# A group's ten transposes in one run over three PSUM banks, and products on two banks

## The chip, the core and the metric

The kernel runs on one core of one Trainium2 chip. The time is that of the device for one execution of the whole program, in microseconds. Engines are named as the profile names them: PE is TensorE, PEld its weight loads, DVE VectorE, ACT ScalarE, POOL GpSimd and SP SyncE.

## What is computed

A recommendation model scores 2048 samples. Each has 50 items of history; their 128-wide rows are gathered from a table, scored against the sample's target by a small network, weighted by a softmax and summed. Five features and their ten pairwise products make a row of 15 × 128 = 1920 numbers, which goes through two cross layers (1920 × 1920) and three dense layers. Cut to what matters:

```python
x = jnp.concatenate([t, seq_emb, t - seq_emb, t * seq_emb], axis=-1)
scores = (jax.nn.relu(x @ aw1 + ab1) @ aw2 + ab2)[..., 0]
weights = jax.nn.softmax(jnp.where(mask, -1e9, scores), axis=1)
hist_feat = jnp.einsum('bs,bsd->bd', weights, seq_emb)
...
for i in range(2):
    xc = dnn_in * (xc @ cross_K[i] + cross_bias[i]) + xc
h = gelu(ln(xc @ w1 + b1)); h = gelu(ln(h @ w2 + b2)); out = sigmoid(h @ w3 + b3)
```

## The kernel before

The batch is cut into 16 tiles of 128 samples, and these into four chunks of four tiles. An opening prepares the rows of chunk 0 and ends at about 324 us. From then on chunk c is multiplied while the histories of chunk c+1 are worked on; chunk 3 has no history beside it.

**Products.** A chunk has 30 steps (two layers of 15 output blocks; `step`, L698) and then a stage for w1. A step makes one block of 128 outputs for 512 samples, in one PSUM bank of 512 columns: `products` (L560) is called three times in a step, for five of the 15 input blocks each, here called the step's first, second and third block of products. Each input block takes three matmuls (L575 to L577), since weights and inputs are split in a high and a low part. Step n writes bank n % 3 of `xps`; DVE reads it in the next step (`x_scale`, L1237), and `x_end` gives the bank back by the semaphore `bank_free`. The fourth bank (`FCB`, semaphore `bank4_free`) serves the small products and the dense layers. In the w1 stage the four tiles each have one of these four banks.

**A group of history.** A tile's 50 items are five groups of ten. In a step that has a group (`p.grp`; 20 of the 30 steps of chunks 0, 1 and 2, in sets of five with a step between the sets), PE transposes the ten gathered blocks `e`: five behind the first block of products and five behind the second (`transposes`, L487, with u = 0 and 1). Both fives go to the same place, `tps` in `aps`, which is guarded by the semaphore `tp_free`: the second five wait until ACT has copied the first to `eT` (`copy_eT`, L780). DVE multiplies the ten copies by the target (`times_target`, L1099) into `teT`; in the next step `hidden` (L509) multiplies both behind the first block of products, and `score` (L524) comes at the step's end. One step later ACT weighs the ten blocks (`weigh`, L810) and DVE sums them (`history`, L1144). The gathers themselves are issued by POOL (L440), a group at a time, when `history` has freed the place.

**Order on ACT.** It is written out in `step` (L954): weight split for the first block (`unit`, which calls `w_hi`, L855), the softmax's exponentials and ten `weigh`, `x_hi` of the previous step (L880, which waits for DVE's `x_end`), the first copy, `unit` for the second block, in some steps a gelu of the dense layers, the second copy, and `unit` for the third. A `w_hi` works three blocks of products ahead. DVE makes the low part of the same weights (`w_lo`, L1212).

**Dense layers.** In steps 2 to 10 of chunks 1, 2 and 3 the dense layers of the chunk before run in between: `fc_turn1` (L643) behind a first block of products, waiting for the norms of DVE (L1278, semaphore `h1n_ready`) and for `FCB`; its gelu on ACT (L894); `fc_w2` (L651) behind the third block, waiting for that gelu; `fc_bias2` on DVE (L1287), which gives `FCB` back.

Of the kernel before, what the change touches and what calls it, by code (L numbers as in the profile page):

```python
# [12 lines left out]
P = 128  # L13
EMB = 128
# [30 lines left out]
SBUFS = 3  # L45
BANKS = 3
EPS = 1e-5
# [94 lines left out]
def build(nc, idx_d, table_d, cate_d, embT_d, rows_d, cols_d, mmw_d, aw1_d, bil_d, kx_d, w1_d, w2_d, out_d, ntiles):  # L142
    assert sum(TILES) == ntiles
    with ExitStack() as ctx:
# [3 lines left out]
        def ps(name, shape):  # L148
            return ctx.enter_context(nc.psum_tensor(name, shape, F32))
# [8 lines left out]

        xps = ps("xps", [P, BANKS + 1, 512])
        FCB = BANKS  # L160
        mps = xps[:, FCB, :]
        aps = ps("aps", [P, 2 * 512])
        tps = aps[:, 0:SUB * P]
        gps = aps[:, SUB * P:(SUB + 1) * P]
        hps = ps("hps", [P, 2 * 512])
        hsum = hps[:, 0:SUB * P]
        hscore = hps[:, SUB * P:SUB * P + GRP]

        spare = xps[:, 0:2, :].rearrange("p k n -> p (k n)")
        tps2 = spare[:, 0:SUB * P]  # L170
        gps2 = spare[:, SUB * P:(SUB + 1) * P]
        hscore2 = xps[:, 2, 0:GRP]

# [197 lines left out]
        lo_final = X1l[:].rearrange("p t f b -> p (t f b)")  # L371

        def raw_slot(w):
            return w % WRING
# [102 lines left out]
        def _(pe):  # L477
# [8 lines left out]

            def transposes(t, g, u):  # L487
                if u == 0:
                    pe.wait_ge(*landed(t, g))
                pe.wait_ge(tp_free, 1).then_inc(tp_free, -1)  # L490
                for s in range(groups(t)[g][1]):
                    last = nc.tensor.transpose(tps[:, s * P:(s + 1) * P], e_sub(t, g, u, s), ident[:])  # L492
                last.then_inc(tp_ready, 1)
# [113 lines left out]
            def w1_products(c):  # L607
                T = TILES[c]
                assert T > 1
                tiles = [b for b in (0, 1, 3, 2) if b < T]  # L610

                whole = FEATS - FINAL if c == CHUNKS - 1 else FEATS
                for k, b in [(k, b) for k in range(whole) for b in tiles]:
                    if b == 0:
# [12 lines left out]
                    m2 = mm(out, xl, Wh[:, s, 0:H1], start=False, stop=(k == FEATS - 1))  # L627
                    if b == 0:
# [3 lines left out]
                    if b == 1:  # L632
                        m0.then_inc(w_free, 1)
                    if k == FEATS - 1 and b == 0:
# [4 lines left out]
                for b in range(T, BANKS):  # L639
                    pe.wait_ge(bank_free, 1).then_inc(bank_free, -1)  # L640

# [37 lines left out]
            def opening_step(p):  # L679
# [18 lines left out]
            def step(p):  # L698
# [8 lines left out]
                if p.grp:  # L707
                    transposes(*p.grp, 0)
# [50 lines left out]
        def _(act):  # L759
# [19 lines left out]

            def copy_eT(u, n=SUB):  # L780
                act.wait_ge(tp_ready, 1).then_inc(tp_ready, -1)
                act.wait_ge(eT_free, 1).then_inc(eT_free, -1)  # L782
                done(af(eT[:, u, 0:n * P], tps[:, 0:n * P], ACT.Copy))  # L783
                act.sem_inc(tp_free, 1)
                act.sem_inc(eT_ready, 1)
# [147 lines left out]
            def opening_step(p):  # L933
# [6 lines left out]
                if p.grp:  # L940
                    n = groups(p.grp[0])[p.grp[1]][1]
                    copy_eT(0, n)
# [11 lines left out]
            def step(p):  # L954
# [18 lines left out]
                if p.grp:  # L973
                    copy_eT(0)
                if p.gate is not None:
# [71 lines left out]
        def _(dve):  # L1047
# [5 lines left out]
            def images():  # L1053
                dve.wait_ge(img_mm, 1).then_inc(img_mm, -1)
                psum = xps[:].rearrange("p k n -> p (k n)").rearrange("p (t n) -> p t n", n=EMB)

# [180 lines left out]
            def x_scale(c, layer, n):  # L1237
                dve.wait_ge(sum_done, 1).then_inc(sum_done, -1)
                dve.wait_ge(mm_done, 1).then_inc(mm_done, -1)
                v.scalar_tensor_tensor(out=fresh(c, layer, n), in0=by_tile(xps[:, n % BANKS, :], c), scalar=col("cb", layer * FEATS + n),  # L1240
                                       in1=fresh(c, layer, n), op0=ALU.add, op1=ALU.mult).then_inc(scaled, 1)
# [62 lines left out]
            def h1_bias(b):  # L1304
                done(v.tensor_tensor(h1[:, b, :], xps[:, b, :], row("b1"), ALU.add))
                dve.sem_inc(bank_free if b < BANKS else bank4_free, 1)

            def h1_rest(c):
                dve.wait_ge(mm_done, 1).then_inc(mm_done, -1)
                for b in range(1, TILES[c]):  # L1310
                    h1_bias(b)
                if TILES[c] < BANKS:
                    dve.sem_inc(bank_free, BANKS - TILES[c])

# [86 lines left out]
            def w1_stage(c):  # L1401
                for k in range(FEATS):
# [4 lines left out]
                    if k == FEATS - 1 and c + 1 < CHUNKS:  # L1407
                        dve.wait_ge(mm_done, 1).then_inc(mm_done, -1)
                        h1_bias(0)
                    unit(c, BLOCKS + k)  # L1410
# [78 lines left out]
            norm2(T - 1)  # L1489
            if T < BANKS:  # L1490
                dve.sem_inc(bank_free, BANKS - T)
            fc_probs(c)
# [50 lines left out]
```

## Time and profile before

| | us |
|---|---|
| median of 3 runs | 2115.8 |
| lowest, highest | 2112.77, 2117.34 |
| the profiled execution | 2113.03 |
| its span | 2111.2 |
| PE busy | 1928.6 (91%) |
| DVE busy | 1337.5 (63%) |
| ACT busy | 914.2 (43%) |
| POOL busy | 894.6 (42%) |

The span runs from the first to the last instruction; 1.8 us of the execution lie around it. A timeline row gives start, duration, engine, line, operation, tiles, sizes, the number of merged instructions, and in brackets the idle time of the engine before it and what ended that; a name with a q (PEq, DVEq) is the engine's own queue, standing at a semaphore. A matmul's shown duration (0.39 us for 512 columns) is longer than the distance to the next one, as matmuls overlap; distances between starts tell what PE can do.

### The profile page before, as it was taken

To read this page: it belongs to the slowest core of one execution; us is meant where nothing else is said; L and a number is where in the kernel's file an instruction comes from. 1 tells how busy PE (TensorE), PEld (TensorE's weight loads), DVE (VectorE), ACT (ScalarE), POOL (GpSimd) and SP (SyncE) were. 2 spreads that over 40 slices of the span, in tenths; PEclk is the share of its full clock that TensorE was granted. 3 is DMA by queue.
4 is the path that set the end of the run, shared out by engine and by line. 5 is a ranking of instruction groups with operands and counts; after the bars stand their busy time and mean duration, and the time that the engine had idled before them with its cause. 6 is when DMAs were issued, how large, how long until landed. Compare 5 with 4: busy or idle time off the path is not lost. (4 is left out here: it accounts for less than half of the span.)

```text
span 2111.2 us, 32903 instructions
## 1 busy us (share of the span) xinstructions
PE 1928.6 (91%) x9608; PEld 1513.0 (72%) x9608; DVE 1337.5 (63%) x2248; ACT 914.2 (43%) x1987; POOL 894.6 (42%) x854
## 2 busy tenths in 40 slices
PE   1666558999999999999999999999999999999997
PEld 1444336777777887777777886777777888888886
DVE  4555564767777755667777755667777654445553
ACT  1433343454544335654444235654445233322234
POOL 7777776556556511555556501555560000000000
PEclk6766669999999999999999999999999999999998
DMA  5112113334434452334434452334332353333320
GB/s 165 50 48 53 50 50 102 104 100 132 117 110 120 144 192 69 99 90 124 125 105 125 142 184 69 99 94 127 118 109 92 111 175 126 89 99 96 98 68 1
DMA packets 99679, 220.31 MB, mean 104 GB/s; under 512 B 21792, under 2 KB 27184, under 8 KB 99376
## 3 DMA queue, kind: packets, MB, share of 16 engines
q1 hardware_dynamic: 63072, 136.90, 21.3%
q0 software_dynamic: 27136, 55.63, 10.5%
q10 hardware_dynamic: 9296, 25.70, 3.3%
q8 instruction: 80, 1.31, 0.3%
q14 instruction: 95, 0.78, 0.1%
HBM read 205.29 MB, written 12.85 MB: 103 GB/s over the span
## 5 line engine op out<-in xcount | busy, mean ns | idle before, releaser
L440 POOL DMA_INDIRECT e<-in_item_table,idx_all x800 | 843.7, 1055 | 650.9 <-issue 302.1
L1212 DVE TENSOR_TENSOR Wl<-raw,Wh 128x640 fp32r<-128x640 f32 (+1 forms) x411 | 331.9, 807 | 267.0 <-DVEq L1211 265.8
L855 ACT ACTIVATE Wh<-raw 128x640 fp32r<-128x640 f32 (+1 forms) x411 | 296.0, 724 | 470.6 <-ACTq L854 467.6
L575 PE MATMUL xps<-X0h,Wh 128*128 128x512 f32 x900 | 364.1, 404 | 1.4 <-PEq L573 1.4
L575 PE MATMUL xps<-X1h,Wh 128*128 128x512 f32 x900 | 359.4, 399 | 0.0
L577 PE MATMUL xps<-X0h,Wl 128*128 128x512 f32 x900 | 351.6, 391 | 0.0
L576 PE MATMUL xps<-X0l,Wh 128*128 128x512 f32 x900 | 351.2, 390 | 0.0
L577 PE MATMUL xps<-X1h,Wl 128*128 128x512 f32 x900 | 351.0, 390 | 0.0
L576 PE MATMUL xps<-X1l,Wh 128*128 128x512 f32 x900 | 350.7, 390 | 0.0
L814 ACT ACTIVATE e<-e,pw 128x128 f32<-128x128 f32 x800 | 242.9, 388 | 15.5 <-ACTq L139 15.5
L577 PEld LDWEIGHTS xps<-X0h,Wl 128*128 128x128 f32 x900 | 169.1, 188 | 37.0
L577 PEld LDWEIGHTS xps<-X1h,Wl 128*128 128x128 f32 x900 | 168.9, 188 | 36.4
L575 PEld LDWEIGHTS xps<-X0h,Wh 128*128 128x128 f32 x900 | 169.5, 188 | 35.4 <-issue 3.5
L575 PEld LDWEIGHTS xps<-X1h,Wh 128*128 128x128 f32 x900 | 169.2, 188 | 33.6 <-issue 1.0
L576 PEld LDWEIGHTS xps<-X1l,Wh 128*128 128x128 f32 x900 | 169.4, 188 | 32.2
L576 PEld LDWEIGHTS xps<-X0l,Wh 128*128 128x128 f32 x900 | 169.7, 189 | 31.1
L1151 DVE TENSOR_REDUCE hist<-e 128x128 f32<-128x1280 f32 (+1 forms) x65 | 155.9, 2399 | 49.5 <-DVEq L1149 49.5
L783 ACT ACTIVATE eT<-aps 128x640 f32<-128x640 f32 x141 | 98.1, 696 | 165.2 <-ACTq L782 164.6
L1103 DVE TENSOR_TENSOR teT<-eT,tT 128x1280 f32<-128x1280 f32 x79 | 117.7, 1490 | 65.2 <-DVEq L1101 65.1
L517 PE MATMUL hps<-eT,A 128*64 128x512 f32 (+2 forms) x640 | 135.9, 505 | 20.0 <-PEq L511 19.9
L492 PE MATMUL aps<-ident,e 128*128 128x128 f32 x700 | 109.3, 289 | 40.4 <-issue 30.4
L521 PE MATMUL hps<-teT,A 128*64 128x512 f32 (+2 forms) x640 | 133.2, 496 | 0.0
(159 smaller groups left out, 2196.7 us busy)
## 6 DMA issues: line engine op xcount, KB each, us to landing
raw<-in_cross_K SPq DMA_DIRECT2D x360, 320.0 KB
raw<-in_w SPq DMA_DIRECT2D x51, 256.0 KB
e<-in_item_table,idx_all POOLq DMA_INDIRECT x800, 2.5
dnn_scratch<-dn ACTq DMA_DIRECT2D x12, 960.0 KB
x1f<-dnn_scratch ACTq DMA_DIRECT2D x3, 2048.0 KB, 9.6
x1f<-dnn_scratch ACTq DMA_DIRECT2D x3, 1792.0 KB, 15.2
e<-in_w SPq DMA_DIRECT2D x9, 256.0 KB, 4.6
dn<-in_embT SPq DMA_DIRECT2D x1, 1024.0 KB, 5.3
```

The lines of the kernel that those rows point to most:

```text
L440: nc.gpsimd.indirect_dma_start(out=dst, out_offset=None, in_=table, in_offset=bass.IndirectOffsetOnAxis(ap=idx_all[:, t, s:s + 1], axis=0) ...
L492: last = nc.tensor.transpose(tps[:, s * P:(s + 1) * P], e_sub(t, g, u, s), ident[:])
L517: last = mm(hsum[u * HID:(u + 1) * HID, a:b], A12[:], eT[:, u, a:b], start=True, stop=False)
L521: last = mm(hsum[u * HID:(u + 1) * HID, a:b], A3[:], teT[:, u, a:b], start=False, stop=True)
L575: m0 = mm(out, wh, Xh[:, 0:T, k, :], start=(k == 0), stop=False)
L576: m1 = mm(out, wh, Xl[:, 0:T, k, :], start=False, stop=False)
L577: m2 = mm(out, wl, Xh[:, 0:T, k, :], start=False, stop=(k == FEATS - 1))
L814: last = af(x, x, ACT.Copy, scale=pw[:, g % 2, s:s + 1])
L855: af(Wh[:, split_slot(w), 0:n], raw[:, rs, 0:n], ACT.Copy).then_inc(hi_done, 1)
L1103: v.tensor_tensor(teT[:].rearrange("p u (s b) -> p (u s) b", b=P), eT[:].rearrange("p u (s b) -> p (u s) b", b=P), tT[:, par:par + 1, :].t ...
L1151: done(v.tensor_reduce(hist[:] if g else acc[:, par, :], x, AX.X, ALU.add))
L1212: v.tensor_tensor(Wl[:, rs, 0:n], raw[:, rs, 0:n], Wh[:, slot, 0:n].bitcast(F32), ALU.subtract).then_inc(lo_done, 1)
```

## The change

The PSUM is one tensor of eight banks. Products alternate between banks 0 and 1; bank 2 is `FCB`; banks 3, 4 and 5 are a place for ten transposes (1280 columns, two and a half banks); 6 and 7 are as before. In a step with a group all ten transposes stand behind the first block of products (`transposes10`), and one ACT instruction of 128×1280 copies them (`copy_eT10`), where the first copy was. Behind the second block none is left. In the w1 stage tile 3 uses bank 3, guarded by `tp_free`, and the tiles are taken in the order 0, 2, 3, 1, so that the bank last used by a step comes last. The opening keeps its form with five and five (`transposes`, `transposes2`), and only its banks have other numbers. The core of the diff:

```diff
-BANKS = 3
+BANKS = 2
+FCB = 2
+TURN = 3
+W1_ORDER = (0, 2, 3, 1)
...
+        turns = flat[:, TURN * 512:(TURN + 3) * 512]
+        tps10 = turns[:, 0:GRP * P]
...
+            def transposes10(t, g):
+                pe.wait_ge(*landed(t, g))
+                pe.wait_ge(tp_free, 1).then_inc(tp_free, -1)
+                for i in range(GRP):
+                    last = nc.tensor.transpose(tps10[:, i * P:(i + 1) * P], e_sub(t, g, i // SUB, i % SUB), ident[:])
+                last.then_inc(tp_ready, 1)
...
-                out = by_tile(xps[:, n % BANKS, :], c)
+                out = by_tile(xps[:, (layer * FEATS + n) % BANKS, :], c)
...
-                tiles = [b for b in (0, 1, 3, 2) if b < T]
+                tiles = w1_order(c)
...
+                    elif k == 0 and b == FCB:
+                        pe.wait_ge(bank4_free, 1).then_inc(bank4_free, -1)
                     elif k == 0:
-                        pe.wait_ge(bank4_free, 1).then_inc(bank4_free, -1)
+                        pe.wait_ge(tp_free, 1).then_inc(tp_free, -1)
...
                 if p.grp:
-                    transposes(*p.grp, 0)
+                    transposes10(*p.grp)
 
                 products(p.chunk, p.layer, p.n, 1)
-                if p.grp:
-                    transposes(*p.grp, 1)
-                elif p.swing is not None:
+                if p.swing is not None:
                     head_turn()
...
+            def copy_eT10():
+                act.wait_ge(tp_ready, 1).then_inc(tp_ready, -1)
+                act.wait_ge(eT_free, 2).then_inc(eT_free, -2)
+                done(af(eT[:].rearrange("p u n -> p (u n)"), tps10, ACT.Copy))
+                act.sem_inc(tp_free, 1)
+                act.sem_inc(eT_ready, 2)
...
                 if p.grp:
-                    copy_eT(0)
+                    copy_eT10()
                 if p.gate is not None:
                     tail_gate()
                 unit(c, 3 * k + 1)
                 if T and 2 <= k < T + 2:
                     fc_gelu1(k - 2)
 
-                if p.grp:
-                    copy_eT(1)
-                elif p.swing is not None:
+                if p.swing is not None:
                     copy_tT(p.swing)
...
             def h1_rest(c):
                 dve.wait_ge(mm_done, 1).then_inc(mm_done, -1)
-                for b in range(1, TILES[c]):
+                for b in w1_order(c)[1:]:
                     h1_bias(b)
```

On PE, in step 9 of chunk 1, from the end of the first block of products to the dense layers' last product (`fc_w3`, on `dn,cols`); L517 and L521 are `hidden`, L492 the transposes. Before:

```order
L521 MATMUL hps<-teT,A 64x128 x2
L492 MATMUL aps<-ident,e 128x128 x5
L575 MATMUL xps<-X0h,Wh 128x512
...
L577 MATMUL xps<-X0h,Wl 128x512
L492 MATMUL aps<-ident,e 128x128 x5
L675 MATMUL xps<-dn,cols 4x128 x8
L575 MATMUL xps<-X0h,Wh 128x512
```

And after:

```order
L532 MATMUL psum<-teT,A 64x128 x2
L503 MATMUL psum<-ident,e 128x128 x10
L586 MATMUL psum<-X0h,Wh 128x512
...
L588 MATMUL psum<-X0h,Wl 128x512
L685 MATMUL psum<-dn,cols 4x128 x8
L586 MATMUL psum<-X0h,Wh 128x512
```

The five transposes that stood behind the second block now stand with the first five, one block of products earlier, and what follows the second block no longer has transposes ahead of it.

On ACT, in step 2 of chunk 1, from `x_hi` (on `X1h`) over the copies (to `eT`), the weight split (to `Wh`) and the gelu (to `dn`) to the third block's split. Before:

```order
L880 ACTIVATE X1h<-x1f 128x4x128
L783 ACTIVATE eT<-aps 128x640
L855 ACTIVATE Wh<-raw 128x640
L894 ACT_TABLE_LOAD
L894 ACTIVATE dn<-xps,cols 128x128 x4
L783 ACTIVATE eT<-aps 128x640
L855 ACTIVATE Wh<-raw 128x640 x2
```

And after:

```order
L895 ACTIVATE X1h<-x1f 128x4x128
L791 ACTIVATE eT<-psum 128x1280
L870 ACTIVATE Wh<-raw 128x640
L909 ACT_TABLE_LOAD
L909 ACTIVATE dn<-psum,cols 128x128 x4
L870 ACTIVATE Wh<-raw 128x640 x2
```

The second copy is gone from behind the gelu, and the first is twice as wide and stands ahead of the weight split and the gelu.

## Rows read from the trace of the kernel before

**Rows 1.** The page: its head, and PE's busy time.

```profile
span 2111.2 us, 32903 instructions
PE 1928.6 (91%) x9608; PEld 1513.0 (72%) x9608; DVE 1337.5 (63%) x2248; ACT 914.2 (43%) x1987; POOL 894.6 (42%) x854
```

**Rows 2.** Waits of PE, 340 to 2085: total us, times, longest.

```profile
PE aps L492 <- PEq L490: 9.9, 9, 1.8
PE xps L648 <- PEq L646: 6.5, 2, 3.5
```

**Rows 3.** Timeline of PE, transposes behind a second block, without a wait.

```profile
811.64 0.39 PE L577 MATMUL xps<-X0h,Wl 128*128 128x512 f32 x1
811.88 0.71 PE L492 MATMUL aps<-ident,e 128*128 128x128 f32 x5
812.34 0.48 PE L575 MATMUL xps<-X0h,Wh 128*128 128x512 f32 x1
812.66 0.39 PE L576 MATMUL xps<-X0l,Wh 128*128 128x512 f32 x1
```

**Rows 4.** Timeline of PE, step 9 of chunk 1, the second five transposes.

```profile
928.66 0.39 PE L577 MATMUL xps<-X0h,Wl 128*128 128x512 f32 x1
930.52 0.74 PE L492 MATMUL aps<-ident,e 128*128 128x128 f32 x5 [1.47 <-PEq L490]
```

**Rows 5.** Timeline of ACT in the same step.

```profile
929.06 0.61 ACT L880 ACTIVATE X1h<-x1f 128x512 fp32r<-128x512 f32 x1
929.58 0.68 ACT L783 ACTIVATE eT<-aps 128x640 f32<-128x640 f32 x1
```

**Rows 6.** Lines by form, ACT, whole span: copies of five transposes, of one.

```profile
L783 ACT ACTIVATE eT<-aps 128x640 f32<-128x640 f32 x139 | 97.2, 699 | 161.8 <-ACTq L782 161.3
L798 ACT ACTIVATE tT<-aps 128x128 f32<-128x128 f32 x13 | 3.6, 278 | 35.2 <-ACTq L797 35.2
```

**Rows 7.** Timeline of ACT and PE, step 3 of chunk 1: gelu, copy, split, `fc_w2`.

```profile
829.27 1.51 ACT L894 ACTIVATE dn<-xps,cols 128x128 f32<-128x128 f32 x4
831.20 0.71 ACT L783 ACTIVATE eT<-aps 128x640 f32<-128x640 f32 x1 [0.42 <-ACTq L782]
832.32 0.74 ACT L855 ACTIVATE Wh<-raw 128x640 fp32r<-128x640 f32 x1 [0.41 <-ACTq L854]
833.14 1.89 PE L656 MATMUL xps<-w,dn 128*128 128x256 f32 x8
```

**Rows 8.** Timeline of DVE and PE from that step to the next `fc_turn1`.

```profile
832.23 1.49 DVE L1103 TENSOR_TENSOR teT<-eT,tT 128x1280 f32<-128x1280 f32 x1 [1.49 <-DVEq L1101]
833.64 0.82 DVE L1212 TENSOR_TENSOR Wl<-raw,Wh 128x640 fp32r<-128x640 f32 x1
842.61 0.63 PE L648 MATMUL xps<-ident,dn 128*128 128x128 f32 x4 [3.04 <-PEq L646]
```

**Rows 9.** Timeline of PE and DVE, steps 1 and 2 of chunk 2.

```profile
1271.15 0.52 PE L492 MATMUL aps<-ident,e 128*128 128x128 f32 x3 [1.37 <-PEq L490]
1276.43 1.92 DVE L1278 TENSOR_SCALAR dn<-dn,fmv,frstd 128x512 f32<-128x512 f32 x4 [0.15 <-DVEq L139]
1278.55 0.60 PE L648 MATMUL xps<-ident,dn 128*128 128x128 f32 x4
```

**Rows 10.** Timeline of PE, last group of chunk 0: waits for its gathers.

```profile
661.77 0.74 PE L492 MATMUL aps<-ident,e 128*128 128x128 f32 x5 [0.55 <-issue]
```

**Rows 11.** Timeline of DVE and PE: a bank's read, and the step after.

```profile
700.31 0.75 DVE L1240 SCALAR_TENSOR_TENSOR x0f<-xps,cols,x0f 128x512 f32<-128x512 f32 x1
705.16 0.39 PE L575 MATMUL xps<-X1h,Wh 128*128 128x512 f32 x1
```

**Rows 12.** Busy time by stretch: PE, PEld, DVE, ACT, POOL, PEclk, DMA share, GB/s.

```profile
822.27:825.65 3.38, 3.38 (x26) 1.90 (x26) 0.29 (x1) 3.38 (x11) 0.00 (x0) 1.00 0.00 0
842.61:847.62 5.01, 5.01 (x25) 2.65 (x26) 0.54 (x1) 3.55 (x11) 2.66 (x3) 0.66 0.20 52
941.72:945.49 3.77, 3.77 (x31) 2.46 (x30) 1.51 (x4) 3.55 (x11) 2.10 (x3) 1.00 0.07 19
```

More of the change, by code:

```diff
@@ L156, in build @@
         img_d = nc.dram_tensor("img_scratch", (ntiles, P, EMB), F32, kind="Internal").ap()
-        xps = ps("xps", [P, BANKS + 1, 512])
-        FCB = BANKS
+        flat = ps("psum", [P, 8 * 512])
+        xps = flat[:, 0:4 * 512].rearrange("p (k n) -> p k n", n=512)
         mps = xps[:, FCB, :]
[L162 to L165, printed above, removed]
+        turns = flat[:, TURN * 512:(TURN + 3) * 512]
+        tps10 = turns[:, 0:GRP * P]
+        tps = turns[:, 0:SUB * P]
+        gps = turns[:, SUB * P:(SUB + 1) * P]
+        hscore2 = turns[:, 2 * 512:2 * 512 + GRP]
+        hps = flat[:, 6 * 512:8 * 512]
         hsum = hps[:, 0:SUB * P]
         hscore = hps[:, SUB * P:SUB * P + GRP]
-        spare = xps[:, 0:2, :].rearrange("p k n -> p (k n)")
+        spare = flat[:, 0:2 * 512]
         tps2 = spare[:, 0:SUB * P]
         gps2 = spare[:, SUB * P:(SUB + 1) * P]
-        hscore2 = xps[:, 2, 0:GRP]
         x_at = -(-nc.sbuf_base // 32) * 32
@@ L371, in build, with w1_order @@
         lo_final = X1l[:].rearrange("p t f b -> p (t f b)")
+        def w1_order(c):
+            return [b for b in W1_ORDER if b < TILES[c]]
         def raw_slot(w):
@@ L484, in images, with transposes @@
                 last.then_inc(img_mm, 1)
-            def transposes(t, g, u):
-                if u == 0:
-                    pe.wait_ge(*landed(t, g))
+            def transposes(t, g):
+                pe.wait_ge(*landed(t, g))
                 pe.wait_ge(tp_free, 1).then_inc(tp_free, -1)
                 for s in range(groups(t)[g][1]):
-                    last = nc.tensor.transpose(tps[:, s * P:(s + 1) * P], e_sub(t, g, u, s), ident[:])
+                    last = nc.tensor.transpose(tps[:, s * P:(s + 1) * P], e_sub(t, g, 0, s), ident[:])
+                last.then_inc(tp_ready, 1)
+            def transposes10(t, g):
+                pe.wait_ge(*landed(t, g))
+                pe.wait_ge(tp_free, 1).then_inc(tp_free, -1)
+                for i in range(GRP):
+                    last = nc.tensor.transpose(tps10[:, i * P:(i + 1) * P], e_sub(t, g, i // SUB, i % SUB), ident[:])
                 last.then_inc(tp_ready, 1)
@@ L609, in w1_products @@
                 assert T > 1
-                tiles = [b for b in (0, 1, 3, 2) if b < T]
+                tiles = w1_order(c)
                 whole = FEATS - FINAL if c == CHUNKS - 1 else FEATS
                 for k, b in [(k, b) for k in range(whole) for b in tiles]:
-                    if b == 0:
+                    if b == tiles[0]:
                         pe.wait_ge(w_ready, 1).then_inc(w_ready, -1)
@@ L627, in w1_products @@
                     m2 = mm(out, xl, Wh[:, s, 0:H1], start=False, stop=(k == FEATS - 1))
-                    if b == 0:
+                    if b == tiles[0]:
                         m0.then_inc(split_free, 1)
@@ L631, in w1_products @@
                             m1.then_inc(x0_free, 1)
-                    if b == 1:
+                    if b == tiles[1]:
                         m0.then_inc(w_free, 1)
-                    if k == FEATS - 1 and b == 0:
+                    if k == FEATS - 1 and b == tiles[0]:
                         m2.then_inc(mm_done, 1)
@@ L637, in w1_products @@
                     m2.then_inc(mm_done, 1)
-                for b in range(T, BANKS):
-                    pe.wait_ge(bank_free, 1).then_inc(bank_free, -1)
             def fc_turn1(j, bank=FCB):
@@ L690, in opening_step @@
                 if p.grp:
-                    transposes(*p.grp, 0)
+                    transposes(*p.grp)
                     transposes2(*p.grp, p.swing is not None)
@@ L707, in step @@
                 if p.grp:
-                    transposes(*p.grp, 0)
+                    transposes10(*p.grp)
                 products(p.chunk, p.layer, p.n, 1)
-                if p.grp:
-                    transposes(*p.grp, 1)
-                elif p.swing is not None:
+                if p.swing is not None:
                     head_turn()
@@ L777, in head_fetch, with copy_eT @@
                 act.dma_start(S[:, b, 3, :], img_d[t]).then_inc(img_landed[b], DMA)
-            def copy_eT(u, n=SUB):
+            def copy_eT10():
[4 more added lines that the diff above has]
+                act.sem_inc(eT_ready, 2)
+            def copy_eT(n):
                 act.wait_ge(tp_ready, 1).then_inc(tp_ready, -1)
                 act.wait_ge(eT_free, 1).then_inc(eT_free, -1)
-                done(af(eT[:, u, 0:n * P], tps[:, 0:n * P], ACT.Copy))
+                done(af(eT[:, 0, 0:n * P], tps[:, 0:n * P], ACT.Copy))
                 act.sem_inc(tp_free, 1)
@@ L941, in opening_step @@
                     n = groups(p.grp[0])[p.grp[1]][1]
-                    copy_eT(0, n)
+                    copy_eT(n)
                     copy_eT2(p.swing, n)
@@ L1054, in images @@
                 dve.wait_ge(img_mm, 1).then_inc(img_mm, -1)
-                psum = xps[:].rearrange("p k n -> p (k n)").rearrange("p (t n) -> p t n", n=EMB)
+                psum = flat[:, 0:ntiles * EMB].rearrange("p (t n) -> p t n", n=EMB)
                 def wide(q):
@@ L1239, in x_scale @@
                 dve.wait_ge(mm_done, 1).then_inc(mm_done, -1)
-                v.scalar_tensor_tensor(out=fresh(c, layer, n), in0=by_tile(xps[:, n % BANKS, :], c), scalar=col("cb", layer * FEATS + n),
+                v.scalar_tensor_tensor(out=fresh(c, layer, n), in0=by_tile(xps[:, (layer * FEATS + n) % BANKS, :], c), scalar=col("cb", layer * FEATS + n),
                                        in1=fresh(c, layer, n), op0=ALU.add, op1=ALU.mult).then_inc(scaled, 1)
@@ L1305, in h1_bias @@
                 done(v.tensor_tensor(h1[:, b, :], xps[:, b, :], row("b1"), ALU.add))
-                dve.sem_inc(bank_free if b < BANKS else bank4_free, 1)
+                dve.sem_inc(bank_free if b < BANKS else bank4_free if b == FCB else tp_free, 1)
             def h1_rest(c):
                 dve.wait_ge(mm_done, 1).then_inc(mm_done, -1)
-                for b in range(1, TILES[c]):
+                for b in w1_order(c)[1:]:
                     h1_bias(b)
-                if TILES[c] < BANKS:
-                    dve.sem_inc(bank_free, BANKS - TILES[c])
             def opening_step(p):
@@ L1408, in w1_stage @@
                         dve.wait_ge(mm_done, 1).then_inc(mm_done, -1)
-                        h1_bias(0)
+                        h1_bias(w1_order(c)[0])
                     unit(c, BLOCKS + k)
@@ L1489, in _ @@
             norm2(T - 1)
-            if T < BANKS:
-                dve.sem_inc(bank_free, BANKS - T)
             fc_probs(c)
```

## The prediction

> **What bounds the kernel now.** I read the page first: PE is busy for 1928.6 of 2111.2 us [rows 1]. What is missing lies mostly in the opening before 324 us, which the change leaves as it is. From 340 us to 2085 us PE hardly stands: the view of waits has nine waits at the transposes, 9.9 us together and at most 1.8, two at `fc_turn1`, 6.5 us, and one for gathers [rows 2, 10]. So only two kinds of things can shorten the run: instructions that leave PE's stream, or those waits. The nine waits are what this change meets. The timeline shows one of them [rows 4, 5]: in step 9 of chunk 1 ACT comes to its first copy only at 929.58, behind ten `weigh` and `x_hi`, and PE, which has been through its second block of products at 928.66, stands until 930.52, because the second five transposes go to the place that this copy empties. PE is not waiting for data that it needs, but for its own output place.
>
> **Part 1, PE's own work.** Sixty groups lose a second run of five transposes and get five more in the first. What an extra run costs is read where none waits [rows 3]: from the last product at 811.64 to the first of the next block 0.70 us, and 0.32 to the one after it, against 0.23 and 0.23 between products (811.64 to 811.88 is about that distance): 1.02 - 0.46 = 0.56 us for the run. What a transpose costs inside a run is the difference between five [rows 3] and four (the run of L648) [rows 9]: 0.71 - 0.60 = 0.11 us, so five more cost 0.55. Saved per group: 0.01 to 0.02 us, about 1 us over 60 groups. A switch from products to transposes and back is nearly free here; this part of the change gives next to nothing. Bounds: 0 (a run is worth its transposes) to 60 x 0.09 = 5 us (if the longer distance at re-entry, 0.32 against 0.23, goes whole). I take 1.0. In chunk 0 even that is lost: its last group waits for its gathers [rows 10], which POOL issues one behind the other, so PE meets the same landing later or earlier. That leaves 0.7.
>
> **Part 2, the nine waits.** They go, as no transposes stand behind a second block any more, and the ten in the first run need a place whose copy was made a step earlier. The idle column understates one of them: 928.66 to 930.52 is 1.86 us where 0.24 is usual [rows 3, 4], so 1.62 us are lost where the row says 1.47; 0.15 more for each. One of the nine, 0.3 us, lies in chunk 0 ahead of the wait for gathers and is worth nothing by the argument above. Eight are left: 9.6 + 8 x 0.15 = 10.8 us. Small ones that the view leaves out may add 0.3: 11.1 us.
>
> **What is late next?** ACT is as late as before and only nobody stands for it there. I followed what stands behind it. The ten transposes end 0.55 us later than five did. The copy of 1280 columns: the line through 128 columns, 278 ns, and 640, 699 ns [rows 6] gives 699 + 640 x 0.82 = 1.23 us, at most twice 0.70 = 1.40 and at least, if the second half came at no cost, 0.70; I take 1.23, since the slope is of the same operation. So in a step with a gelu (8 of these steps have a group) the gelu ends 0.55 + 1.23 - 0.71 = 1.07 us later, at 831.85 instead of 829.27 + 1.51 = 830.78, and PE wants it at 833.14 for `fc_w2` [rows 7]. The margin is 2.4 us before and 1.3 us after: nothing to pay, and if the copy took 1.40, 1.1 us would be left. Were the cover gone, each 0.1 us over it would cost 8 x 0.1 us. The split `w_hi` behind the first copy comes 0.5 to 1.1 us later, and works three blocks of products ahead, over 10 us.
>
> In step 1 of chunks 1 and 2 one wait does come. There DVE's norms feed `fc_turn1` of step 2. Its first norm ends at 1276.43 + 1.92/4 = 1276.91 [rows 9]; behind the later split DVE is late by 1.23 - 0.68 = 0.55, so 1277.46. PE would stand there at 1278.55, less the 1.5 us that it no longer loses at 1271.15 [rows 9], so at 1277.05: 0.4 us of new wait, and by the same rows of chunk 1 some 0.2. I take 0.6 us back.
>
> **Part 3, DVE and the bank of the dense layers.** DVE stands 1.49 us in this step before `times_target` for the second copy [rows 8]. This goes, since both halves now come with the first. The split behind it is then the next to be late: ACT reaches it without the second copy at 831.85 + 0.41 = 832.26 instead of 832.32, ready at 833.0, where DVE took it at 833.64 [rows 7, 8]. So DVE's row of work from there on, up to `fc_bias2`, comes 0.6 us earlier, and `fc_turn1` of step 4, which stands 3.04 us for the bank that this releases [rows 8], stands less by as much. Two such waits, 3.0 and 3.5 us [rows 2]: I take 2 x 0.5 = 1.0 us; bounds 0 and 2 x 1.5.
>
> **Part 4, two banks instead of three.** A step now needs the bank that DVE reads in the step just before. The tightest place I found has the read end at 701.06 and the next step start at 705.16 [rows 11]: 4.1 us of slack. Price nothing; below nothing it can't go, since a third bank releases no one here. The w1 order and the wait on `tp_free` there meet banks idle for several us: nothing. The gathers of chunks 1 and 2 land well ahead; only the group of [rows 10] waits.
>
> **Sum**, against the profiled execution: 2113.0 - 0.7 - 11.1 + 0.6 - 1.0 = 2100.8 us. That execution lies 2.8 us under the median of the three runs, 2115.8, and near the lowest; a median of the changed kernel should then lie between 2100.8 and 2103.6. **I say 2102.**
>
> **The skill against the trace.** Windows that hold nothing but small work between products show how the clock takes it: 3.77 us from `hidden` over the bilinear products to the transposes at a granted clock of 1.00, the 2.4 GHz level [rows 12]. The Trainium skill, TensorE: Matmul & The Clock Gate, Part 4 on the PE-mode transpose, says that transposes don't count as activity of the engine in the way that other matmuls do; by it a longer run of transposes speaks against this change, and the second rival would be the likely case. The trace so far doesn't bear that out.
>
> **Rivals.** *First, the waits come back (0.14).* PE is up to 1.8 us earlier and stands for the same late ACT or DVE a little further on, at `hidden`, `score` or `fc_w2`. For it: ACT is as busy as ever and its first copy starts later. Against it: the margin of 1.3 us [rows 7], and that each of these places lies a whole block of products further on. If all of part 2 came back: 2113 - 1 = 2112; if half, 2107. *Second, slower (0.05): the clock falls behind the longer run.* The same instructions, from `fc_turn1` to the next product, took 3.38 us at clock 1.00 and 5.01 us at 0.66, after the wait of 3.04 us [rows 8, 12]: 1.63 us a fall. The longest stretch of small work grows from 3.77 to 4.3 us, the usual one by the same 0.55. It decides from 12.1/1.63 = 8 falls on, where the gain is eaten, and from 10 the kernel is slower by over 0.2%; at all 60 groups it would be 2101 + 98 = 2199. Against it: 3.77 us did no harm. *Third, more than I say (0.09):* that one fall in the middle vanishes with the shorter wait ahead of it (1.6 us) and the two waits at `fc_turn1` go whole (5.5 us more): 2094. *The change doing nothing on PE* is the first rival with parts 1 and 3 at 0, 2113.
>
> **Chances.** My forecast 0.72, the rivals 0.14, 0.05 and 0.09. The range from 2095 to 2111 takes in the bounds of the copy, of part 1 and of part 3, a first rival by half, and the spread of the runs; it leaves out full return, the clock case and the far end of the third. A measurement can tell about 0.2%, 4.2 us, from no change, so faster means under 2111.6: 0.84; same 0.11; slower 0.05.
>
> **What would show it.** In the profile after: no wait of PE at the ten transposes but the one for gathers near 661 us; ten transposes 1.25 us long between `hidden` and the second block; one copy of 1280 columns at 1.2 to 1.3 us, 60 times; DVE's wait ahead of `times_target` shorter by more than half; the waits at `fc_turn1` near 2.5 and 3.0 us, and two small new ones, 0.2 to 0.4 us, at `fc_turn1` in step 2; the clock at 1.00 from 330 us to the end but for that one fall. The forecast is wrong if the copy takes over 2 us, if PE stands at `fc_w2`, or if windows over the new runs show a clock under 1.

## Result and the profile after

| | us |
|---|---|
| the kernel before, median of 5 runs | 2116.82 (2112.77 to 2118.65) |
| the changed kernel, median of 5 runs | 2102.35 (2101.58 to 2107.81) |
| ratio, with its 95% interval | 0.9934 (0.9922 to 0.9945) |
| the profiled execution of the changed kernel | 2104.58, span 2102.6 |

Five later runs of the changed kernel, beside their own runs of the kernel before, gave 0.9949 (0.9937 to 0.9962), median 2107.89. Single runs of one kernel on one chip differ by 3 to 11 us (`bias_again` below, 2100.29 to 2111.11), so differences of 1 or 2 us are read below from profiles, not from medians.

The page and the waits of PE from 340 to 2085 us, the answer to [rows 1, 2]:

```profile
span 2102.6 us, 32483 instructions
...
PE psum L658 <- PEq L656: 6.9, 4, 3.0
PE psum L658 <- PEq L654: 2.6, 1, 2.6
PE psum L503 <- issue: 0.6, 1, 0.6
```

The nine waits at transposes are gone. Only the wait for gathers is left at the ten (L503, as in [rows 10]), and `fc_turn1` (L658) now waits four times instead of twice in the steps. The row of 2.6 us belongs to the program's last stage, at 2084 us, where the kernel before has a wait of its own (2.92 us at 2092.8) that lay just outside the stretch.

One run of ten transposes with nothing else in it, and the copies, the answer to [rows 3, 6]:

```profile
792.33 0.39 PE L588 MATMUL psum<-X0h,Wl 128*128 128x512 f32 x1
792.56 1.25 PE L503 MATMUL psum<-ident,e 128*128 128x128 f32 x10
793.57 0.48 PE L586 MATMUL psum<-X0h,Wh 128*128 128x512 f32 x1
793.89 0.39 PE L587 MATMUL psum<-X0l,Wh 128*128 128x512 f32 x1
...
L791 ACT ACTIVATE eT<-psum 128x1280 f32<-128x1280 f32 x60 | 73.9, 1232 | 24.7 <-ACTq L790 24.6
```

From 792.33 to 793.57 are 1.24 us and to the next 0.32, less two product distances of 0.23: 1.10 us for ten, where five took 0.56. Two fives are 1.12. The wide copy takes 1232 ns.

Step 3 of chunk 1, the answer to [rows 7, 8], ACT, DVE and PE:

```profile
829.77 1.51 ACT L909 ACTIVATE dn<-psum,cols 128x128 f32<-128x128 f32 x4
831.70 0.74 ACT L870 ACTIVATE Wh<-raw 128x640 fp32r<-128x640 f32 x1 [0.42 <-ACTq L869]
832.54 1.89 PE L666 MATMUL psum<-w,dn 128*128 128x256 f32 x8
832.58 0.82 DVE L1225 TENSOR_TENSOR Wl<-raw,Wh 128x640 fp32r<-128x640 f32 x1 [1.00 <-DVEq L1224]
841.76 0.92 PE L658 MATMUL psum<-ident,dn 128*128 128x128 f32 x4 [2.80 <-PEq L656]
```

The gelu ends at 831.28, 1.26 us ahead of `fc_w2`. DVE stands 1.00 us ahead of the low part for the third block, now for ACT's split.

Where the time went is told by the two middle chunks, each stretch from a chunk's first product to the next chunk's; columns as in [rows 12]. Before:

```profile
778.25:1251.44 473.19, 465.46 (x2396) 365.98 (x2394) 328.46 (x545) 230.01 (x496) 225.51 (x212) 1.00 0.40 118
1251.44:1723.78 472.34, 463.73 (x2396) 365.25 (x2394) 326.48 (x538) 230.24 (x496) 165.25 (x156) 1.00 0.37 111
```

After:

```profile
778.37:1246.22 467.85, 464.58 (x2395) 366.52 (x2394) 328.66 (x545) 225.64 (x476) 227.85 (x212) 1.00 0.40 120
1246.22:1715.40 469.18, 465.47 (x2395) 367.59 (x2394) 326.52 (x538) 226.33 (x476) 167.33 (x156) 0.99 0.37 111
```

Chunk 1 is 5.3 us shorter and chunk 2 only 3.2. Behind the difference is TensorE's granted clock, which goes from its upper level (2.4 GHz, shown as 1.00) to its lower one (1.2 GHz) for some microseconds, here called a fall. Windows over the small work from `fc_turn1` in step 4 on, chunk 1 and chunk 2 of the changed kernel:

```profile
841.76:847.50 5.74, 5.74 (x31) 3.10 (x32) 0.95 (x2) 3.55 (x11) 3.61 (x4) 0.70 0.21 57
1310.20:1317.30 7.10, 7.10 (x31) 3.98 (x32) 1.13 (x3) 3.55 (x11) 2.66 (x3) 0.56 0.13 37
```

After the waits of 2.80 and 3.00 us PE worked at a granted clock of 0.70 and 0.56, between its two levels on the mean of the stretch. Without a fall this work takes 3.38 [rows 12] + 0.55 = 3.93 us to the next product; it took 5.56 and 6.88 in the two chunks. So the falls cost 1.6 and 3.0 us. Before, chunk 1 had one of 1.6 us and chunk 2 none, though its wait there was the longest, 3.50 us (granted clock 1.00 from 1312 to 1325 us). In `two_banks` below, with these same two waits, the clock fell behind both (granted clock 0.50 from 843.75 to 849.5 us and from 1318.73 to 1324, the small work behind the waits). So the 3.0 us that were given back in chunk 2 are a matter of the execution and not of the change.

### The profile page after: what moved, and what is told of

The parts are those of the page before. It is cut to its first block and busy times, and to the rows that moved or that the text cites. A ratio compares the mean times of both kernels' runs of the same rounds, so it can differ in the third digit from the quotient of the medians.

```text
span 2102.6 us, 32483 instructions
## 1 busy us (share of the span) xinstructions
PE 1933.7 (92%) x9608; PEld 1519.9 (72%) x9608; DVE 1336.6 (64%) x2248; ACT 903.2 (43%) x1927; POOL 894.0 (43%) x854
## 5 line engine op out<-in xcount | busy, mean ns | idle before, releaser
L586 PE MATMUL psum<-X0h,Wh 128*128 128x512 f32 x900 | 361.4, 402 | 1.2 <-PEq L584 1.2
L586 PE MATMUL psum<-X1h,Wh 128*128 128x512 f32 x900 | 357.1, 397 | 0.0
L587 PE MATMUL psum<-X0l,Wh 128*128 128x512 f32 x900 | 351.4, 390 | 0.0
L588 PE MATMUL psum<-X0h,Wl 128*128 128x512 f32 x900 | 351.1, 390 | 0.0
L587 PE MATMUL psum<-X1l,Wh 128*128 128x512 f32 x900 | 350.9, 390 | 0.0
L588 PE MATMUL psum<-X1h,Wl 128*128 128x512 f32 x900 | 350.4, 389 | 0.0
L586 PEld LDWEIGHTS psum<-X0h,Wh 128*128 128x128 f32 x900 | 169.4, 188 | 36.5 <-issue 3.3
L588 PEld LDWEIGHTS psum<-X0h,Wl 128*128 128x128 f32 x900 | 169.1, 188 | 36.8
L587 PEld LDWEIGHTS psum<-X1l,Wh 128*128 128x128 f32 x900 | 169.2, 188 | 32.9
L587 PEld LDWEIGHTS psum<-X0l,Wh 128*128 128x128 f32 x900 | 169.6, 188 | 32.0
L528 PE MATMUL psum<-eT,A 128*64 128x512 f32 (+2 forms) x640 | 139.1, 516 | 18.9 <-PEq L522 18.5
L1116 DVE TENSOR_TENSOR teT<-eT,tT 128x1280 f32<-128x1280 f32 x79 | 117.4, 1487 | 41.2 <-DVEq L1114 41.2
```

The costliest lines, as they stand in the source:

```text
L528: last = mm(hsum[u * HID:(u + 1) * HID, a:b], A12[:], eT[:, u, a:b], start=True, stop=False)
L586: m0 = mm(out, wh, Xh[:, 0:T, k, :], start=(k == 0), stop=False)
L587: m1 = mm(out, wh, Xl[:, 0:T, k, :], start=False, stop=False)
L588: m2 = mm(out, wl, Xh[:, 0:T, k, :], start=False, stop=(k == FEATS - 1))
L1116: v.tensor_tensor(teT[:].rearrange("p u (s b) -> p (u s) b", b=P), eT[:].rearrange("p u (s b) -> p (u s) b", b=P), tT[:, par:par + 1, :].t ...
```

## The experiments

Each kernel is the changed one with the edit shown, unless its name says otherwise. Medians of different chips differ, so the ratio to the kernel before on the same chip is what counts.

### Only the banks: `two_banks`

The five and five transposes into one place, with their two copies, are put back; the two product banks and the w1 order stay.

```diff
-                    transposes10(*p.grp)
+                    transposes(*p.grp, 0)
...
                 products(p.chunk, p.layer, p.n, 1)
-                if p.swing is not None:
+                if p.grp:
+                    transposes(*p.grp, 1)
+                elif p.swing is not None:
...
```

> The changed kernel with one part undone: the ten transposes are again five behind the first and five behind the second block of products, into one place, with two copies of 640 columns; products stay on two banks, with the new order in the w1 stage. My theory (the gain is the eight waits of PE for that place): the nine waits are back, 9.5 to 10 us in the view of waits, and the time is that of the kernel before, 2115 to 2118 us, ratio 0.999 to 1.001. Rival (two banks themselves give or cost time): a ratio away from 1, below 0.998 if the banks carry the gain, above 1.002 if PE now stands at bank_free.

Measured: 2115.96 us, ratio 0.9997 (0.9988 to 1.0006), as expected. PE's waits from 340 to 2085 us:

```profile
PE psum L497 <- PEq L495: 9.8, 9, 1.8
PE psum L659 <- PEq L657: 6.6, 2, 3.5
PE psum L497 <- issue: 0.6, 1, 0.6
```

These are rows 2 and 10 of the kernel before again, in number and size. No wait at `bank_free` is among them. Two banks and the new order cost nothing and give nothing that 0.1% would show.

### The wait away, nothing merged: `own_banks`

Four transposes behind the first block in bank 3, six behind the second in banks 4 and 5, with semaphores and a copy of their own. (Two places of five would share bank 4 between a write of PE and a read of ACT with nothing to order them, so four and six it is.)

```diff
-                for i in range(GRP):
+                for i in range(4):
...
+            def transposes6(t, g):
+                pe.wait_ge(tp2_free, 1).then_inc(tp2_free, -1)
+                for i in range(4, GRP):
...
+                if p.grp:
+                    copy_eT6()
...
```

> The changed kernel without the merging: four transposes behind the first block of products in bank 3, six behind the second in banks 4 and 5 with semaphores of their own, copied by two instructions, the second behind the gelu as in the kernel before. No transpose waits for a copy of its own step. My theory (waiting for the place is what was lost): the waits at transposes go, nearly the whole gain is there, 10.5 to 11.5 us less than before, 2105 to 2107 us; DVE still stands for the second copy (60 to 65 us at times_target), so the two waits at fc_turn1 stay at 3.0 and 3.5 us and no small ones come in step 2. Rival (the gain is in one run, one copy and one switch fewer): 2115 to 2117 us.

Measured: 2107.50 us, ratio 0.9959 (0.9946 to 0.9973), 8.9 us less than the kernel before on its chip, where I expected 10.5 to 11.5. PE's waits from 340 to 2080 us, and chunks 1 and 2:

```profile
PE psum L664 <- PEq L662: 6.2, 2, 3.4
PE psum L534 <- PEq L532: 1.0, 2, 0.7
PE psum L503 <- issue: 0.5, 1, 0.5
```

```profile
777.95:1246.33 468.38, 464.76 (x2396) 366.07 (x2395) 328.50 (x545) 228.99 (x496) 226.05 (x212) 1.00 0.41 120
1246.33:1715.03 468.70, 464.98 (x2395) 366.39 (x2394) 326.77 (x538) 229.09 (x496) 168.42 (x156) 1.00 0.37 111
```

With the two halves apart and only the place doubled, chunks 1 and 2 take together 937.1 us, as the changed kernel's 937.0. That is not yet like with like, since here too the clock fell behind the two waits at `fc_turn1` (L664). In the time line of PE:

```profile
841.03 1.09 PE L664 MATMUL psum<-ident,dn 128*128 128x128 f32 x4 [2.87 <-PEq L662]
...
845.67 0.48 PE L592 MATMUL psum<-X0h,Wh 128*128 128x512 f32 x1
...
1310.10 0.63 PE L664 MATMUL psum<-ident,dn 128*128 128x128 f32 x4 [3.38 <-PEq L662]
...
1315.00 0.48 PE L592 MATMUL psum<-X0h,Wh 128*128 128x512 f32 x1
```

The small work takes 4.64 and 4.90 us, where by [rows 12], with four transposes for five, it would take 3.38 - 0.11 = 3.27: the falls cost 1.4 and 1.6 us, 3.0 in all, and 4.6 in the changed kernel. Without them 934.1 stand beside 932.4. So the waits for the place were nearly all of the gain, and for the merging and the order that comes with it these profiles leave 1.7 us in two chunks, out of 11.5 (the kernel before takes 945.5 less its one fall of 1.6). In the times the ratio's interval begins just above the first of the changed kernel's (0.9922 to 0.9945) and overlaps with the second (0.9937 to 0.9962): a small gain by merging is likely, and isn't shown. As expected the two waits at `fc_turn1` stay near the old sizes (2.9 and 3.4 us) and none comes in step 2. Not expected were two waits of 0.7 and 0.3 us in `hidden` (L534), ahead of its last 128 columns, for the semaphore `hscore_free`, which DVE gives when it has read the scores of the group before: PE, earlier by up to 1.8 us, is there first.

### The copy: `two_copies` and `three_copies`

```diff
-                done(af(eT[:].rearrange("p u n -> p (u n)"), tps10, ACT.Copy))
+                done(af(eT[:, 0, :], tps10[:, 0:SUB * P], ACT.Copy))
+                done(af(eT[:, 1, :], tps10[:, SUB * P:GRP * P], ACT.Copy))
```

> The changed kernel with the ten transposes copied by two instructions of 640 columns, one behind the other, each waited for. ACT needs 2 x 0.70 us and a gap for a wait more, some 0.5 us per group. My theory (the copy lies in a margin of 1.3 us ahead of fc_w2): 2102 to 2104 us, no wait at fc_w2, the two small waits in step 2 longer by about 0.5 us each. Rival (the single copy carries a part of the gain): 60 x 0.1 us or more, 2108 us and up.

Measured: 2104.84 us, ratio 0.9945 (0.9931 to 0.9958), with no wait at `fc_w2`, as expected; the time is just above the 2102 to 2104 that I gave. ACT has some 0.3 us per group more (two copies of 0.70 us and a gap against one of 1.23), and PE meets little of it: in its profile the two waits in step 2 are 0.65 and 1.00 us instead of 0.36 and 0.71, and three of 0.2 to 0.4 us have come in `hidden`. The ratio overlaps with both sets of the changed kernel, so the single copy is no part of the gain that can be told.

`three_copies` makes the copy of 1280 columns three times.

> The changed kernel with the copy of 1280 columns made three times, each waited for: ACT is 2.8 to 3.3 us later behind it in each of 60 groups. It measures the cover that I gave the copy. Theory (1.3 us ahead of fc_w2 at 8 places, 2.0 us ahead of hidden at the tightest, none ahead of the norms in step 2): PE stands 1.5 to 2 us at 8 fc_w2, 3 us at 2 fc_turn1, up to 1 us at some six hidden: 20 to 26 us in all, 2121 to 2130 us. Rivals: ACT sets the pace (60 x 3): 2280 us; or the cover is far wider than I think: under 2108 us.

Measured: 2221.70 us, ratio 1.0506 (1.0490 to 1.0522), some 120 us slower than the changed kernel and about five times what I expected. PE's waits from 340 to 2085 us:

```profile
PE psum L528 <- PEq L522: 25.6, 22, 2.4
PE psum L528 <- PEq L526: 22.6, 13, 3.0
PE psum L666 <- PEq L664: 14.2, 8, 1.8
PE psum L658 <- PEq L656: 13.9, 6, 3.5
PE psum L586 <- PEq L584: 10.9, 3, 3.6
PE psum L638 <- PEq L629: 5.5, 2, 2.8
```

At the place that I had priced the price is right: eight `fc_w2` (L666) wait 1.8 us each, where I expected 1.5 to 2. The two further copies take 2.7 us (1.36 from start to start), 1.5 more than the cover of 1.26. But `fc_turn1` (L658) waits six times, not twice, `hidden` (L528), where I allowed six waits under 1 us, waits 35 times, 48 us in all; three times PE waits at a layer's first output block for the inputs just made (L584, 3.6 us each); and the clock falls nine times between 560 and 1600 us. The waits come to 92.7 us here and to 7.5 in the changed kernel ahead of its last stage. What I missed: ACT late makes DVE late, DVE's part of the next step starts late, and ACT waits for it there. ACT's wait for the softmax's maxima from DVE, in the changed kernel and here, 340 to 2085 us:

```profile
ACT corr L821 <- ACTq L819: 50.3, 40, 3.2
ACT corr L823 <- ACTq L821: 137.5, 40, 6.8
```

A delay in each step is not measured against the cover of one step; here it reached places at which PE doesn't wait in the changed kernel.

### A longer run: `long_run`

```diff
-                for i in range(GRP):
+                for i in (*range(GRP), *range(GRP)):
```

> The changed kernel with each of the ten transposes made twice in the same run (the same values at the same place): 20 transposes, 1.09 us more in each of 60 groups. It measures what a transpose costs inside a run and whether a run of small work of 5.7 us lets the clock fall. Theory: 0.109 us each, clock 1.00 over these runs: 2102 + 65 + 1 to 3 for waits at the gelu and the norms = 2168 to 2171 us. Rival (a long run of transposes makes the clock fall, 1.6 to 3 us each, at up to 48 places): 2190 to 2310 us.

Measured: 2165.15 us, ratio 1.0240 (1.0226 to 1.0255). By the ratios that is 65 us more than the first set of the changed kernel, 1.08 per group; the time itself is a little under the 2168 to 2171 that I expected. The run of twenty in the step with the longest small work, and the window over that work (`hidden`, bilinear products, twenty transposes):

```profile
969.78 2.35 PE L503 MATMUL psum<-ident,e 128*128 128x128 f32 x20
```

```profile
966.48:971.88 5.40, 5.40 (x45) 4.09 (x45) 3.03 (x4) 3.44 (x11) 3.93 (x5) 1.00 0.16 45
```

Ten more cost 2.35 - 1.25 = 1.10 us, and the clock stays at 1.00 over 5.4 us of small work. The only falls of this run between 340 us and the last stage lie again at the two waits at `fc_turn1` (2.61 and 3.02 us). So runs of twenty transposes didn't bring the clock down; where it fell, PE had been standing. The Trainium skill, TensorE: Matmul & The Clock Gate, Part 4 on the PE-mode transpose, says that they don't count as activity in the way other matmuls do; no run here shows a cost of that.

### The two waits that are left: `bias_first`, `bias_again`

In step 4 PE waits at `fc_turn1` for a bank that `fc_bias2` releases, late in DVE's step. The edit moves that call to the step's start.

```diff
+                if T and 3 <= k < T + 3:
+                    fc_bias2(k - 3)
                 if c and k == 0:
                     r_lo(c, FEATS - 1)
...
-                if T and 3 <= k < T + 3:
-                    fc_bias2(k - 3)
```

> The changed kernel with one call moved on DVE: fc_bias2, which releases the bank of the dense layers, stands at the start of its step instead of behind the softmax, the weights' low part and x_scale. My theory of the two waits left at fc_turn1 in step 4 (2.8 and 3.0 us, each followed by a fall of the clock): PE stands for a bank that DVE could release 3 us earlier; they shrink to under 0.3 us and the falls go with them, 1.6 to 3 us each: 2092 to 2097 us. Rival (DVE as a whole is late there, its earlier work sets the time): the waits shrink by under 1 us and the time stays at 2100 to 2103.

Measured: 2101.74 us, ratio 0.9933 (0.9920 to 0.9947), not the 2092 to 2097 that I expected but in the rival's range. PE's waits from 340 to 2080 us, in part:

```profile
PE psum L666 <- PEq L664: 4.1, 2, 2.1
...
PE psum L658 <- PEq L656: 1.1, 2, 0.7
```

The waits at `fc_turn1` of step 4 are gone, and 2.0 and 2.1 us have come at `fc_w2` of the same step, which waits for ACT's gelu. ACT came late to it because DVE gave it the softmax's maxima late: the last of them ends at 842.30, and ACT, which had stood for it, then works with no stop above 0.41 us to the gelu's end at 853.12.

```profile
842.40 1.28 ACT L821 ACT_TABLE_LOAD   x1 [3.92 <-ACTq L819]
```

Of 5.8 us of waiting 1.7 went. Its profile shows no fall of the clock in the chunks, and both take 465.4 and 465.5 us. I took that for a reason to run it again.

> bias_first once more beside the changed kernel. Theory: the waits of step 4 are 2.0 and 2.1 us, at fc_w2, too short for the clock to fall behind them, so chunks 1 and 2 together are 5 to 6 us shorter than in the changed kernel where that has its falls, and 1 us where it has none; the time is 0 to 6 us less, 2096 to 2103 us. Rival (the first profile's clock was luck): the falls are there as well, and the time is equal within 1 us.

Measured: 2102.46 us, ratio 0.9933 (0.9917 to 0.9949). Waits and sizes are the same, yet chunks 1 and 2 take 470.0 and 468.5 us:

```profile
850.33 3.13 PE L666 MATMUL psum<-w,dn 128*128 128x256 f32 x8 [1.98 <-PEq L664]
```

```profile
850.33:857.50 7.17, 7.17 (x23) 6.12 (x24) 4.01 (x11) 1.96 (x3) 4.53 (x4) 0.55 0.15 37
```

Here the clock did fall behind a wait of 1.98 us. So the rival holds in what it says of the clock: that of the first profile was luck. Whether `bias_first` is faster than the changed kernel stays open: on this chip its median is 5.4 us lower, but the intervals of the ratios overlap. The same program's chunks 1 and 2 took 930.9 us in one execution and 938.4 in another, with the same waits, by falls alone: 4.6 us in chunk 1 and 3.0 in chunk 2.

### Moving DVE's work: `aim_later`, `aim_norms`

```diff
-            fetch, aim, swing = s - 6, s - 4, s - 1
+            fetch, aim, swing = s - 6, s - 2, s - 1
```

> The changed kernel with one number changed: the target's preparation on DVE (head_aim, 3.1 us) stands two steps ahead of a tile's first group instead of four, so it leaves step 3, where DVE also has the dense layers' statistics. bias_first moved the wait at fc_turn1 in step 4 to fc_w2 of the same step (2.0 and 2.1 us), so DVE's and through it ACT's lateness is the cause, not the place of fc_bias2. Theory: with DVE 3 us earlier at step 4 both waits go (5.8 us) and with them the falls of the clock behind them (1.9 and 3.0 us in the changed kernel's profile): 2092 to 2097 us, PE standing 340 to 2085 us under 5 us in all. Rival (the wait only moves to step 5 or 6, where head_aim now stands): 2100 to 2103 us with new waits there.

Measured: 2110.58 us, ratio 0.9979 (0.9965 to 0.9993): slower than the changed kernel. PE's waits, 340 to 2085 us:

```profile
PE psum L638 <- PEq L629: 3.8, 2, 2.2
PE psum L528 <- PEq L522: 3.0, 2, 1.7
PE psum L528 <- PEq L526: 1.5, 2, 0.9
PE psum L658 <- PEq L656: 1.4, 3, 0.7
...
```

The waits of step 4 shrank to 0.3 us, and others took their place: `head_aim` of a chunk's first tile now stands at the end of step 29, and DVE frees that step's bank late for the w1 stage (L629); that of the second tile makes `times_target` late (L522). One more wait grew at chunk 0's start, 3.33 us at 331.65 instead of 1.23 at 330.48 in the changed kernel. The waits moved, as the rival said, but not to steps 5 and 6, and the time is above its 2100 to 2103 too.

`aim_norms` adds to this that in step 1 the square roots stand ahead of `x_hi` and the norms behind `times_target`.

> aim_later, and in step 1 of each chunk the square roots on ACT stand ahead of x_hi and the norms on DVE behind times_target, each two to three instructions earlier. Theory: the two small new waits at fc_turn1 of step 2 (0.36 and 0.71 us) come from the later weight split behind the wide copy and go; 1 us less than aim_later, 2091 to 2096 us, below what a comparison of times can tell, so the view of waits decides. Rival: the norms in front of the weight split make that late, and a wait at fc_w2 or a product comes instead.

Measured: 2106.89 us, ratio 0.9965 (0.9950 to 0.9979), above the 2091 to 2096 that I gave, as it keeps the waits of `aim_later`. In its view of waits `fc_turn1` has one wait of 0.3 us left, where `aim_later` had three, 1.4 us in all. The one that is left is that of step 4; the small waits of step 2 do come from where I said, and moving the norms removes them with no new wait at `fc_w2` or at a product.

### Once more, and all moves inside a step: `after_again`, `all_early`

> The changed kernel once more, on the same chip as the two beside it. It tells the spread of times from run to run. Theory: 2101 to 2105 us, ratio 0.993 to 0.995 to the kernel before; in its profile the waits are where they were (0.4 and 0.7, 2.8 and 3.0 us at fc_turn1), and falls of the clock stand behind the last two.

Measured: 2107.89 us, ratio 0.9949 (0.9937 to 0.9962), the waits as before, and a fall of the clock at each of the two at `fc_turn1`. The ratio is within the 0.993 to 0.995 that I gave; the time is outside the 2101 to 2105, and three of its five runs are.

`all_early` is `bias_first`, with `head_aim` and, in step 1, the norms between `times_target` and the low part for the third block. The norms' square roots on ACT stand ahead of `x_hi` in that step, which is not shown here.

```diff
                 if p.grp:
                     times_target(p.grp[0])
+                if p.aim is not None:
+                    head_aim(p.aim)
+                if T and k == 1:
+                    fc_norms1(T)
...
```

> bias_first with two more moves on DVE inside their steps: head_aim ahead of the weights' low part for the third block (where DVE stands 1.0 us), and in step 1 the norms there too, with their square roots ahead of x_hi on ACT. Unlike aim_later no work goes to another step. Theory: DVE comes to step 4 some 1.3 us earlier, the wait at fc_w2 falls from 2.0 to 0.8 us and those in step 2 go, 3 to 4 us less than bias_first in chunks 1 and 2: 2094 to 2100 us. Rival (the late low part of the weights is then waited for, or DVE passes its lateness on): no less than bias_first.

Measured: 2096.41 us (2095.99 to 2099.44), ratio 0.9903 (0.9889 to 0.9917), as expected. Waits in part, and chunks 1 and 2:

```profile
...
PE psum L666 <- PEq L664: 1.9, 2, 1.2
...
```

```profile
780.42:1243.93 463.51, 462.42 (x2396) 366.29 (x2394) 328.30 (x545) 225.57 (x476) 226.75 (x212) 1.00 0.41 121
1243.93:1707.48 463.55, 462.29 (x2396) 366.45 (x2394) 326.76 (x538) 225.97 (x476) 163.80 (x156) 1.00 0.38 113
```

The waits at `fc_w2` are 0.7 and 1.2 us, those in step 2 are gone, and no clock falls in the chunks: 927.1 us against 937.0, and against 930.9 in the profile of `bias_first` without falls. It beats the kernel before and the changed one. That short waits save the falls too is what the profile suggests. The other profiles fit: in all thirteen no fall between 340 us and the last stage stands at a wait shorter than 1.98 us. That is a count and not yet a rule, since longer waits, up to 3.50 us, passed without a fall.

## Why the prediction was right

**What bounds.** Right. PE is the bound, and the waits at the transposes were waits for a place: `own_banks` removes them alone and has nearly all of the gain, `two_banks`, which brings them back and keeps the banks and the order, has none.

**Part 1, a switch is nearly free.** Right: 1.10 us for ten against 2 x 0.56, 0.02 us a group. Chunk 0, where the gathers set the last group, is 0.8 us shorter, from 454.4 to 453.6 us. I had given it nothing; the wait for gathers grew by only 0.1 us.

**Part 2, the waits, 11.1 us.** Right: all nine are gone.

**What is late next.** The gelu: 1.29 us of margin expected, 1.26 found; the copy 1.23 us by the line, 1.232 measured across three banks. The two new waits in step 2 were named but sized too small: 0.2 and 0.4 us expected, 0.36 and 0.71 found:

```profile
1271.77 1.92 DVE L1291 TENSOR_SCALAR dn<-dn,fmv,frstd 128x512 f32<-128x512 f32 x4 [0.15 <-DVEq L142]
1272.62 0.63 PE L658 MATMUL psum<-ident,dn 128*128 128x128 f32 x4 [0.71 <-PEq L656]
```

My first norm ended a quarter into the four, at 0.48 us, and PE started at once. One such instruction takes 0.55 us (four overlap within the 1.92), and PE starts 0.30 us after its end. The term was 0.6 us, and is 1.1.

**Part 3, DVE and the bank.** The mechanism was right, the size smaller: 3.04 and 3.50 us became 2.80 and 3.00, 0.7 us instead of 1.0. DVE's wait ahead of `times_target` fell from 65.1 us to 41.2 in the whole span, which is less than half. But 38.0 and 37.2 us of it are in the opening, which the change doesn't touch. From 340 to 2085 us it fell from 27.1 us to 4.0, as I said, before and after:

```profile
DVE teT L1103 <- DVEq L1101: 27.1, 28, 2.7
DVE teT L1116 <- DVEq L1114: 4.0, 9, 0.4
```

**Part 4, banks.** Right, by `two_banks`.

**The sum.** In the profiles: 12.2 us expected, 8.4 measured (2113.03 to 2104.58). The gap is the clock, 3.0 us for the longer and additional fall behind the two waits, and 0.9 us by which the opening ended later; smaller misses cancel. With the falls taken off, chunks 1 and 2 gained 11.5 us (943.9 to 932.4), and the 0.7 that are missing are mostly the waits in step 2 (0.5) and part 3 (0.3). I had counted the one fall of the kernel before as a constant, with a chance that it would vanish, and not the chance that a second would come. The median of 2102.35 beside my 2102 owes something to luck: the second set of runs has 2107.9.

**Rivals.** The waits coming back: not for the changed kernel, but it is what happened to my own improvements, `bias_first` and `aim_later`. The clock falling behind long runs of transposes: no, by `long_run`. By the letter one of my signs of being wrong did come, a run of ten under a lower clock:

```profile
1315.68 1.64 PE L503 MATMUL psum<-ident,e 128*128 128x128 f32 x10
```

It takes 1.64 us instead of 1.25, but it stands in the fall behind the wait of 3.00 us, which had begun before this run; I should have left such windows out of the sign.

## What to carry to other kernels

When the bounding engine waits, look whether it waits for data or for its own output place. Here a second place, or asking for it a step earlier, gave back nearly the whole wait, while merging instructions that stream back to back anyway was worth little. Before moving work to shorten the next wait, ask which engine is late: where DVE handed its lateness to ACT and ACT to PE, moving a release mostly moved the wait, and moving work into another step did the same; work moved within the step, into time in which that engine stands, did help.

## What the runs showed of the hardware

A wait of 2 to 3.5 us of PE may cost as much again through the clock: falls behind such waits cost 1.4 to 4.6 us, and come in one execution and not in the next of the same program (930.9 and 938.4 us for the same two chunks). In the thirteen profiles all 26 falls between 340 us and the last stage begin during a wait of 1.98 us or more, or within 1.5 us of its end. Small work, fp32 transposes among it, didn't do that: 5.4 us of it ran at clock 1.00. An ACT copy out of PSUM across three banks takes what a line through shorter ones gives, 1232 ns for 1280 columns. An fp32 transpose of 128×128 costs 0.11 us within a run, and a run of five or ten between products at most 0.02 us beyond that.
